# Four-layer gated cross-attention network on one Trainium2 core: routed rows gathered inside the third attention, weights loaded one stage ahead, semaphores cleared by ranges

## The reference

```python
x = x + tanh(g_xattn[i]) * xattn_i(layernorm(x), ctx)
x = x + tanh(g_ffn[i]) * ffn_i(layernorm(x))
```

## Time and profile before

| what | value |
|---|---|
| median of 3 runs | 5703.66 us (5700.96 to 5715.34) |
| the profiled execution, its own time | 5709.04 us |
| its span in the profile | 5707.3 us |
| mean granted clock of TensorE | 0.929 of full speed |
| PE busy | 4836.8 us, 85% of the span |
| DVE busy | 3943.6 us, 69% |
| ACT busy | 2707.8 us, 47% |
| POOL busy | 2171.1 us, 38% |

### The profile page before, as it was taken

How to read it: one execution, slowest core, us unless ns; L and a number is a source line. 1 busy time by engine, 2 the same in 40 slices (tenths; PEclk the granted TensorE clock), 3 DMA queues, 4 the chain that set the end, 5 groups by cost and what they waited for, 6 DMA issues and landing times. The chain is left out here.

```text
span 5707.3 us, 133493 instructions
## 1 busy us (share of the span) xinstructions
PE 4836.8 (85%) x41659; PEld 3572.5 (63%) x41659; DVE 3943.6 (69%) x9897; ACT 2707.8 (47%) x5454; POOL 2171.1 (38%) x3095
## 2 busy tenths in 40 slices
PE   7998988999933995099989989888998799998898
PEld 4665658888822663066656657766776577776554
DVE  5776857777755332277767758888886799897544
ACT  4665755555510332066645545555554455554344
POOL 5442001011146002655533347777776533333200
PEclk9998989999965998599999989999999899998878
DMA  1004100000021442100000000000000000000000
GB/s 39 8 5 204 51 13 6 5 5 5 5 68 57 136 138 92 46 8 6 4 13 1 0 10 0 0 0 0 0 0 6 8 2 2 2 2 5 1 13 17
DMA packets 108941, 140.24 MB, mean 25 GB/s; under 512 B 35832, under 2 KB 83256, under 8 KB 103996
## 3 DMA queue, kind: packets, MB, share of 16 engines
q1 hardware_dynamic: 100544, 120.88, 6.3%
q0 software_dynamic: 8192, 16.79, 1.0%
HBM read 47.44 MB, written 58.72 MB: 19 GB/s over the span
## 5 line engine op out<-in xcount | busy, mean ns | idle before, releaser
L2180 POOL TENSOR_TENSOR l3a_probs<-l3a_probs,l3a_later 128x512 f32<-128x512 f32 x256 | 320.6, 1281 | 4.9 <-DVE l3a_total L2368 4.9
L2166 POOL TENSOR_TENSOR l3a_keys<-l3a_kT,head 128x2048 f32<-128x2048 f32 x64 | 230.4, 3600 | 232.4 <-ACT l3a_kT L2293 232.4
L1595 POOL DMA_INDIRECT l1c_rows<-l_rows,l1f_slots x128 | 122.5, 957 | 443.0 <-PEq L1587 402.4
L170 POOL TENSOR_TENSOR l1x_ve<-l1x_mv,eps 128x1 f32<-128x1 f32 x64 | 12.1, 190 | 659.9 <-DVE l1x_mv L162 659.9
L2228 PE MATMUL l3a_scores<-l3a_keys,l3a_qT 128*128 128x512 f32 x512 | 255.2, 601 | 4.2 <-POOL l3a_keys L2166 4.2
L1666 POOL TENSOR_TENSOR l2f_hid<-l2f_prod,l2f_route 128x512 f32<-128x512 f32 x128 | 152.2, 1194 | 256.6 <-DVE l2f_prod L1813 246.7
L298 PE MATMUL l3a_po<-l3a_vals,l3a_probsT 128*128 128x32 f32 x2048 | 248.0, 270 | 0.2
L254 ACT ACTIVATE l3a_probs<-l3a_probs 128x512 f32<-128x512 f32 x256 | 161.6, 631 | 182.1 <-DVE l3a_probs L245 177.0
L298 PEld LDWEIGHTS l3a_po<-l3a_vals,l3a_probsT 128*128 128x128 f32 x2048 | 246.9, 192 | 0.7 <-ACT l3a_probsT L279 0.4
L1514 PE MATMUL l1e_h<-l1e_xhi,l1f_parts 128*128 128x512 f16 x640 | 205.0, 382 | 9.6 <-DVE l1e_gated L1572 8.1
L2166 POOL TENSOR_TENSOR l3c_keys<-l3c_kT,head 128x1232 f32<-128x1232 f32 x64 | 144.0, 2250 | 156.7 <-ACT l3c_kT L2293 156.7
(11 more groups left out here) (581 smaller groups left out, 17124.0 us busy)
## 6 DMA issues: line engine op xcount, KB each, us to landing
l_rows<-l0f_zeros SPq DMA_DIRECT2D x34, 1024.0 KB, 26.2
l1f_parts<-l1f_split SPq DMA_DIRECT2D x40, 512.0 KB, 3.6
l1e_x_in<-l_rows SPq DMA_DIRECT2D x40, 256.0 KB, 2.8
l1f_down<-l1f_w SPq DMA_DIRECT2D x40, 256.0 KB, 2.3
l_rows<-l1e_y_out SPq DMA_DIRECT2D x40, 256.0 KB, 2.7
l1f_w<-in_L_W SPq DMA_DIRECT2D x16, 256.0 KB, 3.3
out_x<-x_res SPq DMA_DIRECT2D x16, 256.0 KB, 2.0
x_res<-in_x SPq DMA_DIRECT2D x1, 3840.0 KB, 12.5
```

The costliest lines, as they stand in the source:

```text
L2166: pool.tensor_tensor(keys[it.par][:, :, :, :], kT[it.par][:, :, :].unsqueeze(2).to_broadcast([P, J, G4, T]), g.head32[:, :].unsqueeze(1).u ...
L2180: pool.tensor_tensor(v, v, later[:, :].unsqueeze(1).to_broadcast([P, 4, T]), ALU.mult).then_inc(s_masked, 1)
```

## The change

1. The stage `l1c` is gone. Its gathers and its additions stand in the attention `l2x` (`routed=True`): POOL's word `rows` issues two gathers in each slot, and DVE's words `row0` and `row1` add one row each. All other steps of `l2x` are one group later than before (`late`), and `rest` on POOL also waits for gathers that have landed. POOL's queue in `l2x` is written out in full, those of the other engines for 8 groups instead of 6.
2. Each stage function is now a generator that first allocates its weights and yields the list of its loads. SP of the stage before issues them (`load_ahead`), at the front of its queue or behind the stage's own loads. In `l1e` it stands in front of the tile loads. Stages take their SBUF in turn from the left and from the right, and `l3_y` and `l3_z` are there for the whole kernel.
3. `Stage.__exit__` clears semaphores by ranges of neighbouring numbers.
4. The four lists of the small-head attention are new, for `l0x` and for `l2x`. In PE's, `scoreA` and `shiftB` are neighbours, `mtA` comes behind `turn2`, and `v0` stands behind `scoreB`.

```diff
@@ Stage.__exit__
-                    for s in self.sems:
-                        pool.sem_clear(s)
+                    nums = sorted(s.num for s in self.sems)
+                    for i, first in enumerate(nums):
+                        if i == 0 or nums[i - 1] != first - 1:
+                            until = first
+                            while until in nums:
+                                until += 1
+                            pool.sem_clear(range(first, until))
+def load_ahead(sp, g):
+    for dst, src, sem in g.ahead:
+        sp.dma_start(dst, src).then_inc(sem, 16)
@@ small_head_attention, POOL, context_rest
+                    if routed:
+                        for j, t in enumerate((it.b + 2, it.b + 2, it.b + 1, it.b + 1)):
+                            for u in (min(t, n - 1), min(t, n - 1) - 1):
+                                if u >= 0:
+                                    pool.wait_ge(g.s_rows[u % 2][j], 32 * (u // 2 + 1))
@@ POOL
+                def gather(it, j):
+                    p = it.par
+                    if (due := nth(it, GROUP, j, ago=2)) is not None:
+                        pool.wait_ge(s_comb, 2 * due)
+                    for k in range(2 * j, 2 * j + 2):
+                        pool.indirect_dma_start(
+                            rows[p][:, k * P:(k + 1) * P], None, g.xs[:, :],
+                            bass.IndirectOffsetOnAxis(ap=g.slots[:, it.b * CHOICES + k:it.b * CHOICES + k + 1], axis=0)
+                        ).then_inc(g.s_rows[p][j], 16)
+                order = ["maxA s1 value0 maxB s2 rows",
+                         "bias maxA maxB value1 rows s3",
+                         "maxA deviation maxB rest rows",
+                         "maxA maxB next rows"]
@@ PE
+                order = ["weigh2-2 scoreA shiftB-1 turn0-1 turn_o-2 v1 output-2 scoreB turn1-1 turn2-1 mtA weigh0-1 shiftA mtB weigh1-1",
+                         "weigh2-2 scoreA shiftB-1 turn0-1 turn_o-2 x output-2 scoreB turn1-1 turn2-1 q mtA weigh0-1 shiftA mtB weigh1-1",
+                         "weigh2-2 scoreA shiftB-1 turn0-1 turn_o-2 k output-2 scoreB turn1-1 turn2-1 mtA weigh0-1 shiftA mtB weigh1-1",
+                         "weigh2-2 scoreA shiftB-1 turn0-1 turn_o-2 output-2 scoreB v0 turn1-1 turn2-1 mtA weigh0-1 shiftA mtB weigh1-1"]
@@ DVE
+                def combine(it, j, c):
+                    k = 2 * j + c
+                    x = g.x[:, bass.ts(it.b * GROUP + j, P)]
+                    if c == 0:
+                        dve.wait_ge(g.s_rows[it.par][j], loads(it, 2))
+                    else:
+                        dve.drain()
+                    if k == CHOICES - 1:
+                        fr.statistics_free(dve, it)
+                    dve.scalar_tensor_tensor(x, rows[it.par][:, k * P:(k + 1) * P], g.route[:, bass.ds(it.b * CHOICES + k, 1)], x,
+                                             ALU.mult, ALU.add).then_inc(s_comb, 1)
+                order = ["rest2-2 v0 row0-2 divide-2 maxA row1-2 add-2 rest0-1 maxB rest1-1",
+                         "rest2-2 row0-2 v1 divide-2 maxA row1-2 add-2 rest0-1 maxB rest1-1 stats",
+                         "rest2-2 row0-2 q divide-2 maxA row1-2 add-2 rest0-1 maxB rest1-1",
+                         "rest2-2 k row0-2 divide-2 maxA row1-2 add-2 rest0-1 maxB norm rest1-1"]
@@ run_experts (l1e), SP
+                load_ahead(sp, g)
                 skewed(sp, TILES, [(load, 0), (store, 3)], TILES)
-def combine(nc, g, outer, n, slots, route):
...
```

More of the change, by code:

```diff
@@ L108, in sb @@
     def sb(self, name, shape, dtype=F32):
-        return self.ctx.enter_context(self.nc.sbuf_tensor(f"{self.name}_{name}", list(shape), dtype))
+        return self.ctx.enter_context(self.nc.sbuf_tensor(f"{self.name}_{name}", list(shape), dtype, side=self.side))
     def sb2(self, name, shape, dtype=F32):
@@ L324, in statistics @@
             dve.wait_ge(self.s_ve, due)
+    def statistics(self, dve, it, free=False):
+        if not free:
+            self.statistics_free(dve, it)
         for j in range(GROUP):
@@ L597, in at, with slots @@
             return slice(j * P, (j + 1) * P)
-        def slots(steps, order):
+        def slots(steps, lags, order):
             out = []
             for j in range(GROUP):
-                for step, lag, ago in [steps[k] for k in order[j].split()]:
-                    out.append((lambda it, f=step, j=(j - ago) % GROUP: f(it, j), lag + (1 if j < ago else 0)))
+                for word in order[j].split():
+                    name, _, ago = word.partition("-")
+                    if name in steps:
+                        b = j - int(ago or 0)
+                        out.append((lambda it, f=steps[name], j=b % GROUP: f(it, j), lags.get(name, 2) + late - b // GROUP))
             return out
@@ L695, in add_bias @@
                     pool.tensor_tensor(x, x, bvo_s[:, :].unsqueeze(1).to_broadcast([P, GROUP, P]), ALU.add).then_inc(s_bo, 1)
[L697 to L700, removed]
-                       "s1": (lambda it, j: spread(it, 1), 2, 0), "s2": (lambda it, j: spread(it, 2), 2, 0),
-                       "s3": (lambda it, j: spread(it, 3), 2, 0)}
@@ L703, in _ @@
-                steps.update(one)
-                skewed(pool, n, slots(steps, ["maxA maxB s1", ("bias " if biased else "") + "maxA s2 maxB value1 s3",
-                                              "maxA deviation maxB rest", "next maxA maxB value0"]), 6)
+                def gather(it, j):
[7 more added lines that the diff above has]
+                        ).then_inc(g.s_rows[p][j], 16)
@@ new lines, in _ @@
+                steps = {"maxA": lambda it, j: split_max(it, j, 0), "maxB": lambda it, j: split_max(it, j, 1),
+                         "deviation": lambda it, j: fr.inverse_deviation(pool, it), "rest": lambda it, j: context_rest(it),
+                         "value0": lambda it, j: value_rest(it, 0), "value1": lambda it, j: value_rest(it, 1),
+                         "next": lambda it, j: spread(it, 0), "s1": lambda it, j: spread(it, 1),
+                         "s2": lambda it, j: spread(it, 2), "s3": lambda it, j: spread(it, 3)}
@@ L707, in _ @@
+                skewed(pool, n, slots(steps, lags, order), n if routed else 6)
             @block.tensor
@@ L1003, in _ @@
                 for u in range(3):
-                    steps[f"rest{u}"] = (lambda it, j, u=u: rest(it, j, u), 2, 1)
-                fronts = [("v1 ", " stats"), ("", " q"), ("", " k"), ("v0 ", " norm")]
-                skewed(dve, n, slots(steps, ["divide maxA rest0 add maxB " + mid + "rest1 rest2" + end for mid, end in fronts]), 6)
+                    steps[f"rest{u}"] = lambda it, j, u=u: rest(it, j, u)
+                if routed:
+                    steps["row0"], steps["row1"] = lambda it, j: combine(it, j, 0), lambda it, j: combine(it, j, 1)
@@ L1037, in _ @@
             def _(sp):
-                for dst, src in weights:
-                    sp.dma_start(dst, src).then_inc(s_w, 16)
+                load_ahead(sp, g)
                 sp.wait_ge(s_zeros, 1)
```

285 lines of the change are left out of this document (141 added, 144 removed), and 3 rows, old and new, of the table order.

## The result

The changed kernel takes 5584.8 us (median of 4, 5568.2 to 5590.0) against 5708.6 for the kernel before on the same chip: ratio 0.9775, 95% interval 0.9763 to 0.9786. It is faster by 124 us where 213 were forecast (from 5703.7 to 5491, range 5455 to 5540). Its profiled execution took 5590.0 us.

A forecast was written before the change was run, and what follows sets the result against it. PE's queue was taken to set the pace of both attentions, with no PE work between `l1e` and `l2x`. From 5709.0, -170.0 - 23.9 - 29.0 + 4.8 + 12.5 - 14 + 7 = -212.6, less 5.4, gave 5491 us (5455 to 5540).

The forecast's parts named there:

- stage that goes: Between `l1e`'s last store and `l2x`: 174.0 us lie there today, 4.0 would remain; -170.0 us.
- clears, weights ahead: Between stages and at their starts: range clears save 23.9 us, weights loaded a stage ahead save 29.0 us.
- loads in front of `l1e`: In `l1e`, SP issues the nine loads of `l2x` before the first tile, which engines await; +4.8 us.
- filling `l2x`: Start of `l2x`: first score 35 us behind the start instead of 22.4, after 22 gathers on POOL; +12.5 us.
- `l0x`: New lists in `l0x`: two fewer tile-shape borders a slot save 12.2 us; taken as -14, ends 0 and -20.
- groups of `l2x`: Steady groups of `l2x`, with new lists, gathers and additions: 28.8 us instead of 28.35; +7, ends -18 and +58.
- it should be near 27.2: In `l0x`, a group of 28.1 us should take about 27.2 us with the new lists.
- From the 27.4 of PE I go up to 28.8: In `l2x`, PE would need about 27.4 us a group, raised to 28.8 for stalls; +7 us.
- my rivals: Whole kernel: gathers hidden 5460 (0.22), DVE/POOL bound 5526 (0.20), plumbing does less 5515 to 5520 (0.04), gathers in chain 5812 (0.01).
- new waits eat it: End of the `l0x` list estimate where new waits cancel the saved borders: 0 instead of -14 us.
- a pair of gathers in front of the maxima: In `l2x`, a 2.6 us gather pair on POOL holds up `maxA` or `maxB`, for which `mtA` and `mtB` wait.
- a clear's time goes with its width or is that of one: Range clears between stages: gain nil if time goes with width, 24 us if that of one; -23.9 taken.

The follow-up runs named there:

- e1: The changed kernel with 64 more instructions (128 already satisfied waits) in PE's queue at the start of `l0x`; 5504.5 us.
- e2: The changed kernel with PE's queue in `l0x` and `l2x` written out in full instead of a loop; 5509.0 us.
- e5: The kernel before with 248 more satisfied waits in PE's queue at the start of `l0x` and 245 at that of `l2x`; 5806.2 us.
- e9: e1 with `mtA` moved back between `scoreB` and `turn1` in all four slots of PE's list; 5535.0 us.
- e17: e1 without the 128 additions of routed rows and their drains, gathers kept; 5507.9 us in a single execution.
- e13: The kernel of e9 run again on another chip; 5507.3 us.
- e14: The kernel of e11 run again on another chip; 5527.0 us.
- e11: e1 with the semaphores cleared one by one again, as in the kernel before; 5581.6 us.

## Why the prediction was wrong

| step | forecast | measured | |
|---|---|---|---|
| stage that goes | -170.0 | -170.3 | 3.7 us from the store to `l2x` (4.0 taken) |
| clears, weights ahead | -52.9 | -48.6 | all stages but `l0x`, `l1e` and `l2x`, with the end; 21.8 of it are rows of clears (26.2 us before, 4.3 after) |
| loads in front of `l1e` | +4.8 | +5.3 | first tile 6.3 us behind SP's first load |
| filling `l2x` | +12.5 | +14.5 | 2283.59 - 2246.71 = 36.9 (35 taken) |
| `l0x` | -14 | +37.9 | fetches +42.6 (after against e1), the rest -4.7 |
| groups of `l2x` | +7 | +42 | fetches +27 (after against e1), additions and clock +15 |

**The step that failed** is the one that gave both attentions a pace for all their groups, from the slot's instructions alone: "it should be near 27.2" in the part on `l0x`, and "From the 27.4 of PE I go up to 28.8" in the part on `l2x`. A loop that had fetched nothing was taken to go on fetching nothing, when PE's program ahead of it had changed length. 42.6 + 27 of the 94 us between forecast and result are this, shown by e1 and e2 in one direction and by e5 in the other. Why the fetches come back at some places and not at others stays open. None of my rivals names it. The page of before had the line for q8, but I asked no question of it. The Trainium skill (Runtime: NRT & Kernel Launch, "Instruction fetch mechanics") has a fetch in pieces of 256 instructions, agreed here by the records between packets, and a stall for a jump out of what is held; I hadn't weighed it. It puts what is held at two pieces for all engines in one sentence and at 2048 instructions for PE in another. The loops of before jump back over six pieces without a packet, which rules out the first for PE here and agrees with the second.

**The lists.** The borders were counted rightly: `scoreA` and `shiftB` follow each other without a border, and `turn_o` comes 0.11 behind `turn0`, where it came 0.22 behind a score. What was measured without the fetches, -4.7, lies near the end "new waits eat it", not at the -14 that I took. The wait was not the `output` behind `turn_o` that I named but `turn1` behind DVE's `add`, in a bank that `y_p` shares, now that no `mtA` stands between. e9 gives the forecast pace back, 27.0 and 27.3, with one border less than the list that was forecast.

**`l2x`.** That an addition waits about 0.25 us was right as a mean (0.22), that DVE and POOL have room was right, and 28.8 for a group was 0.3 short of 29.1 ahead of the loop. But the mechanism was another, and so near a number is partly luck: the group pays for one addition, the `row1` in front of `add` that meets POOL's bias, and not for a pair of gathers in front of the maxima, as I had argued. e17 and the two timelines show it.

**Clears.** The number nearly held (21.8 us for 23.9), but the choice that it rested on, a clear's time goes with its width or is that of one, was a false one. It grows with the width, from 38 ns for one to 70 for 5 and 136 for 18, and stays far below the 0.065 us apiece of single clears.

**Weights ahead.** The starts came as forecast (`l0f`, `l1x` within 0.1 us of the stage's start, L1127 and L1934 above). `l3f` was no shorter: it took 323 us in the kernel after at a clock of 0.78, 322 in the one before, and 306 in e1 at 0.83. Over all the traces here it takes 305 to 331 us. What sets it no run shows, no step of mine held it, and it can shift a whole time by as much.

## What to carry to other kernels

Before forecasting an edit ahead of a long loop, look whether the program's DMA queue is silent while it turns: if so, its pace can hang on where the loop begins, and the edit can take that away (10 us a turn here) without touching it. To test for it, move the loop by 64 instructions (128 satisfied waits here) or write it out; both are a few lines. A list order that saves borders between tile shapes must be checked for which wait the removed neighbour had filled; and where one list serves two stages, give each its own, as the same edit gave 13 us in `l0x` and cost 8 in `l2x`. And a mean wait per instruction does not say what a group pays: look at which of the instructions wait, and whether PE's work stands behind them.

## What the hardware showed that I had not expected

- A clear of a range of semaphores takes longer with its width, but little: 70 ns for 5, 136 for 18, and at most 283 in this kernel, where single clears follow each other by 65 ns and take 38.
- A jump back over 98 KB of PE's program (1567 records, 256 to 16 KB) costs nothing that can be seen at some places, and 6.7 to 7.0 us of stall in two parts (first turns of `l0x`, after and e5) at others; at one and the same place (`l2x` in e5) three jumps went the one way and one the other.
- PE's clock fell from 2.4 to 1.2 GHz for 3.4 us at a time inside `l2x`, behind its filling: nine times in e13, where PE waits longer (slot 1 takes 9.9 us ahead of the loop instead of 8.25), never in e14. What such a fall costs, apart from the waits that come with it, no run here separates.
- A 128x128 addition of 0.35 us took up to 1.84 us where it met a POOL instruction, and ended 0.15 us behind it.
- One kernel's `l2x` took 561 us on one chip and 511 on another (e11, e14), with `l0x` at 491 and 490 and `l3a` at 952 on both.
